# Gate scores folded into existing products, and phase 1 reordered, in a fused conv-and-MoE kernel

## What is computed

```
x: (16, 56, 56, 96) float32
# block 1, on windows of 7x7 tokens, after a layer norm of x over the 96 channels
w  = _ln(windows(_ln_c(x)), ln1_w, ln1_b)
xB = w @ Bm ;  h[t] = xB[t] + h[t-1] @ A   for the 49 places of a window ;  xr = h @ Cm
y  = gelu(_ln(xr, ln2_w, ln2_b) @ W1 + b1) @ W2 + b2          # 96 -> 384 -> 96
x2 = x + xr + y
# block 2: 4 experts, the best 2 of a token
t      = (x2 - mean) / sqrt(var + 1e-5)
scores = t @ gate_w + gate_b                                   # 96 -> 4
probs  = softmax(scores), kept for the top 2, divided by their sum
out    = x2 + sum_e probs_e * (gelu(t @ w1[e] + b1[e]) @ w2[e] + b2[e])
```

## Time and profile before

| | |
|---|---|
| median of three executions | 2178.2 us |
| the profiled execution: its time | 2182.9 us |
| the profiled execution: its span | 2181.2 us |
| granted clock of TensorE, mean | 0.982 |
| PE busy | 2028.1 us (93%) |
| DVE busy | 1606.3 us (74%) |
| ACT busy | 1465.5 us (67%) |
| POOL busy | 1451.7 us (67%) |
| DMA | 272.89 MB, 125 GB/s |

### The profile page before, as it was taken

One profiled execution on the slowest core, in us unless ns is written; L12 is line 12 of the kernel. 1 busy time (PEld: TensorE's weight loads), 2 busy tenths in 40 slices (PEclk: granted clock), 3 DMA queues, 4 the chain that ended last, 5 costly groups with the idle time before them and its releaser, 6 DMA issues.

```text
span 2181.2 us, 39083 instructions
## 1 busy us (share of the span) xinstructions
PE 2028.1 (93%) x10145; PEld 1437.0 (66%) x10145; DVE 1606.3 (74%) x6863; ACT 1465.5 (67%) x2529; POOL 1451.7 (67%) x1286
## 2 busy tenths in 40 slices
PE   3999999999999999999965999999999999999996
PEld 2656565666666666666644777777777777777775
DVE  5677777777777777777744777777777777777775
ACT  3555555545455555555523888988898888898895
POOL 2366666666666666666553777777777777777776
PEclk9999999999999999999976999999999999999998
DMA  4011111121112111111115666676667667666663
GB/s 161 28 54 58 54 50 62 49 63 47 63 47 63 50 60 52 58 54 44 40 43 188 202 215 206 199 216 207 203 207 211 206 201 213 203 207 214 208 203 94
DMA packets 120721, 272.89 MB, mean 125 GB/s; under 512 B 25702, under 2 KB 34303, under 8 KB 120500
## 3 DMA queue, kind: packets, MB, share of 16 engines
q1 hardware_dynamic: 85680, 209.91, 32.4%
q0 software_dynamic: 32000, 58.87, 7.7%
q10 hardware_dynamic: 2820, 1.61, 0.3%
HBM read 204.28 MB, written 66.98 MB: 124 GB/s over the span
## 4 chain that ended last, share of the span: by engine, by line
PE 52%; POOL 20%; DVE 20%; issue 6%; ACT 1%; DMA 1%; ACTq 0%; SPq 0%; POOLq 0%; DVEq 0%
POOL rstd L396 11%; POOL sorted_rows L405 7%; PE mix_ps L1035 7%; PE mix_ps L1033 6%; PE mix_ps L1034 6%; DVE xr_n L625 4%; PE up_ps L1019 3%; PE turn_ps L1019 3%; PE turn_ps L1020 3%; DVE stats L613 3%; PE up_ps L1020 3%; PE turn_ps L1021 3%; PE up_ps L1021 3%; PE tok_ps L1042 3%; DVE y_lo L701 3%
## 5 line engine op out<-in xcount | busy, mean ns | idle before, releaser
L436 POOL DMA_INDIRECT out<-out_sb,idx x412 | 423.8, 1029 | 263.9 <-DVE out_sb L832 155.4
L788 DVE TENSOR_TENSOR g_lo<-g,g_hi 128x512 fp32r<-128x512 f32 x618 | 420.3, 689 | 207.8 <-ACT g_hi L546 117.7
L405 POOL DMA_INDIRECT sorted_rows<-rows,pos x392 | 421.7, 1076 | 114.1 <-issue 99.9
L546 ACT CAST g_hi<-g 128x512 fp32r<-128x512 f32 x618 | 380.9, 616 | 13.1
L485 ACT ACTIVATE g<-up_ps 128x512 f32<-128x512 f32 x294 | 175.6, 597 | 253.3 <-PE up_ps L891 134.5
L425 POOL TENSOR_TENSOR ex<-euler,rows 128x16 f32<-128x16 f32 x103 | 311.9, 3028 | 14.2 <-DMA rows<-sorted_rows 13.0
L900 PE MATMUL y_ps<-g,d_raw 128*96 128x512 f32 x588 | 298.3, 602 | 0.2 <-ACT y_sb L492 0.2
L396 POOL TENSOR_TENSOR rstd<-var_eps,neg_half 128x8 f32<-128x8 f32 x147 | 248.6, 1691 | 12.2
L1033 PE MATMUL mix_ps<-g_hi,ew 128*96 128x512 f32 x618 | 244.5, 396 | 0.5 <-DVE g_lo L788 0.5
L1035 PE MATMUL mix_ps<-g_lo,ew 128*96 128x512 f32 x618 | 244.2, 395 | 0.0
L1034 PE MATMUL mix_ps<-g_hi,ew 128*96 128x512 f32 x618 | 244.0, 395 | 0.0
(11 more groups left out here) (159 smaller groups left out, 4426.7 us busy)
## 6 DMA issues: line engine op xcount, KB each, us to landing
ew<-expert_w SPq DMA_DIRECT2D x206, 384.0 KB
ew<-expert_w SPq DMA_DIRECT2D x206, 288.5 KB
rows<-sorted_rows SPq DMA_DIRECT2D x103, 394.0 KB
x_in<-in_x SPq DMA_DIRECT2D x49, 384.0 KB
out<-out_sb,idx POOLq DMA_INDIRECT x412
sorted_rows<-rows,pos POOLq DMA_INDIRECT x392
sorted_rows<-pad_rows SPq DMA_DIRECT2D x11, 394.0 KB, 10.4
expert_w<-w_hi SPq DMA_DIRECT2D x4, 192.0 KB, 2.6
```

The source lines that it names most:

```text
L405: pool.indirect_dma_start(out=sorted_rows[:, :], out_offset=bass.IndirectOffsetOnAxis(ap=pos[:, r, s:s + 1], axis=0), in_=rows[:, r, s, :] ...
L436: pool.indirect_dma_start(out=out_rows, out_offset=bass.IndirectOffsetOnAxis(ap=idx[:, r, s:s + 1], axis=0), in_=out_sb[:, r, s, :], in_of ...
L546: act.copy(g_hi[:, n % PART_RING, :], g[:, n % G_RING, :]).then_inc(hi_done, 1)
L788: dve.tensor_tensor(g_lo[:, n % PART_RING, :], g[:, n % G_RING, :], f(g_hi[:, n % PART_RING, :]), ALU.subtract).then_inc(lo_done, 1)
```

## The change

It alters phase 1 alone (and the place of columns within a row: x2, then the four scores, then the normalised t, then the number of the token).

- **Scores.** The gate weights, with their mean over channels taken off (`centred_weights`), are multiplied on the chip into Cm, W2, A, Bm and b2 as four more columns: sum_xr gives 104 columns (xr, the scores of xr, and the scores of the normalised x), down and turn_y give 100. VectorE multiplies the scores of x back by the deviation (`dev_x`), sums up (`take_xr`, `add_x2`), multiplies by LN_T's rstd and adds the bias (`gate`). The transposes of the normalised rows, tn_t and the score products are gone.
- **xr in PSUM.** The copy of xr is gone: bn_stats and the adds read mix_ps, and ScalarE normalises xr out of mix_ps (`normalise_xr`). The mix region is free when both have read it.
- **Rows.** Four of the eight sub-tiles are normalised on ScalarE (`normalise_rows`, a period later), four on VectorE.
- **Order.** from_input follows from_state ahead of the ups, sum_xr follows rank; the copy to h_t comes before gelu 0. y_lo comes before add_x2, positions after taking xr.
- **GpSimd.** var_eps is made by VectorE; one power over 16 columns serves LN_X and LN_T; all 8 scatters stand together.
- **Loads.** Eight first loads (with turned_w, Cm and W2 transposed), three for the MLP, two late ones.

```diff
-            def rstd_of(k, t, used):
-                pool.wait_ge(moment_ok[k], t + 1)
...
-                pool.tensor_scalar(var_eps[:, k, :], moment[:, k, :, 1], LN_SCALE[k], LN_EPS[k], ALU.mult, ALU.add).then_inc(
-                    var_ok[k], 1)
...
+            def rstd_of_r(t):
+                pool.wait_ge(var_ok[LN_R], t + 1)
...
+                pool.tensor_tensor(rstd_r[:, t % 2, :], var_eps[:, LN_R, :], neg_half[:, 0, :], ALU.pow).then_inc(rstd_r_ok, 1)
+
+            def rstd_of_x_and_t(t):
...
+                pool.tensor_tensor(rstd_xt[:, t % 2, :, :], var_eps[:, LN_X:, :], neg_half[:, :, :], ALU.pow).then_inc(rstd_xt_ok, 1)
...
-                if tile(p - 1):
-                    rstd_of(LN_T, p - 1, tn_ok)
-                if tile(p + 3):
-                    rstd_of(LN_X, p + 3, x_n_ok)
-                if tile(p - 2):
-                    scatter(p - 2, (0, 1, 2))
-                if tile(p + 1):
-                    rstd_of(LN_R, p + 1, xr_n_ok)
-                if tile(p - 2):
-                    scatter(p - 2, (3, 4, 5, 6, 7))
+                if tile(p + 1):
+                    rstd_of_r(p + 1)
+                if tile(p + 3) or tile(p - 1):
+                    rstd_of_x_and_t(p + 3)
+                if tile(p - 2):
+                    scatter(p - 2, range(SUBS))
...
+            def normalise_xr(t):
+                act.wait_ge(shift_r_ok, t + 1)
+                if t >= 1:
+                    act.wait_ge(xr_turned, t)
+                for s in range(SUBS):
+                    ins = act.activation(xr_n[:, s, :], mix_tok[:, s // HALF_SUBS, s % HALF_SUBS, 0:C], ACT.Identity,
+                                         scale=rstd_r[:, t % 2, s:s + 1], bias=shift_r[:, s:s + 1])
+                ins.then_inc(xr_n_ok, 1)
+
+            def normalise_rows(t):
+                act.wait_ge(shift_t_ok, t + 1)
+                for s in range(HALF_SUBS, SUBS):
...
+                ins.then_inc(t_n_ok, 1)
...
-                    gelu(p, 0)
-                    gelu(p, 1)
                 if tile(p + 2):
                     normalise_x(p + 2, 0)
                 if tile(r):
...
-                    act.copy(h_t[:, :], mix_ps[0:C, :]).then_inc(h_t_ok, 1)
+                    act.copy(h_t[:, :], mix_ps[0:CG, :]).then_inc(h_t_ok, 1)
+                if tile(p):
+                    gelu(p, 0)
+                    gelu(p, 1)
+                if tile(p + 2):
+                    normalise_x(p + 2, 1)
+                if tile(p - 2):
+                    normalise_rows(p - 2)
                 if tile(p):
                     gelu(p, 2)
                     gelu(p, 3)
...
                     copy_y(p, 0)
                     gelu(p, 4)
-                if tile(p - 1):
...
-                    act.copy(tn_t[0:C, :], turn_ps[0:C, :]).then_inc(tn_t_ok, 1)
+                if tile(r):
+                    normalise_xr(r)
                 if tile(p):
                     gelu(p, 5)
...
+            def take_xr(t):
+                dst = x_xr[:, t % 2, :, :].rearrange("p (b s) c -> p b s c", b=2)
...
+                dve.tensor_tensor(dst[:, :, :, C:CG], mix_tok[:, :, :, CG:CGX],
+                                  dev_x[:, t % DEV_RING, :].rearrange("p (b s) -> p b s", b=2).unsqueeze(3).to_broadcast(
+                                      [P, 2, HALF_SUBS, EXPERTS]), ALU.mult).then_inc(in_gate_ok, 1)
+                dve.tensor_tensor(dst[:, :, :, 0:C], mix_tok[:, :, :, 0:C],
+                                  x_in[:, t % X_RING, :, :].rearrange("p (b s) c -> p b s c", b=2), ALU.add)
+                dve.wait_ge(in_gate_ok, t + 1)
+                dve.tensor_tensor(dst[:, :, :, C:CG], mix_tok[:, :, :, C:CG], dst[:, :, :, C:CG], ALU.add).then_inc(x_xr_ok, 1)
...
             for p in periods():
                 r = p + 1
-                if tile(p - 1):
-                    add_x2(p - 1, 1)
                 if tile(p):
                     dve.wait_ge(y_hi_ok, p + 1)
                     dve.tensor_tensor(y_lo[:, :], turn_ps[0:C, :], f(y_hi[0:C, :]), ALU.subtract).then_inc(y_lo_ok, 1)
-                if tile(p - 2):
-                    positions(p - 2)
                 if tile(p - 1):
+                    add_x2(p - 1, 1)
                     dve.wait_ge(x2_ok, 2 * p)
-                    moments(LN_T, p - 1, rows[:, (p - 1) % ROW_RING, :, COL_X2:COL_T])
+                    in_stats(LN_T, p - 1, lambda s: rows[:, (p - 1) % ROW_RING, s, COL_X2:COL_BELOW])
+                    variance(LN_T, p - 1, (rstd_xt_ok, p + 3))
...
                 if tile(r):
                     dve.wait_ge(xr_summed, r + 1)
-                    dve.tensor_copy(xr[:, :, :].rearrange("p (b s) c -> p b (s c)", b=2), mix_tok).then_inc(xr_copied, 1)
-                    dve.wait_ge(xr_copied, r + 1)
-                    moments(LN_R, r, xr)
...
+                    in_stats(LN_R, r, lambda s: mix_tok[:, s // HALF_SUBS, s % HALF_SUBS, 0:C])
+                    variance(LN_R, r, (rstd_r_ok, r))
+                    take_xr(r)
+                    shift_of_r(r)
+                if tile(p - 2):
+                    positions(p - 2)
                 if tile(p):
                     add_x2(p, 0)
-                if tile(r):
-                    if r >= 1:
-                        dve.wait_ge(xr_turned, r)
-                    normalise(LN_R, r, xr_n, xr).then_inc(xr_n_ok, 1)
+                if tile(p + 3) or tile(p - 1):
+                    dve.wait_ge(rstd_xt_ok, p + 4)
+                if tile(p + 3):
+                    shift_of_x(p + 3)
                 if tile(p - 1):
+                    shift_of_rows(p - 1)
                     gate(p - 1)
+                    normalise_rows(p - 1)
...
             def from_state(r):
-                mix.take(pe, h_t_ok, r + 1)
...
                 if r >= 1:
                     pe.wait_ge(h_t_ok, r)
+                    pe.wait_ge(x_xr_ok, r)
+                    pe.wait_ge(xr_n_ok, r)
...
                 if tile(r):
                     from_state(r)
+                    from_input(r)
                 if tile(p):
                     up(p, 0)
                     up(p, 1)
...
                 if tile(r):
-                    from_input(r)
+                    sum_xr(r)
...
-                if tile(p - 1):
-                    turn.take(pe, tn_t_ok, p)
-                    pe.wait_ge(tn_ok, p)
-                    to_channels(rows[:, (p - 1) % ROW_RING, :, COL_T:COL_BELOW]).then_inc(tn_turned, 1)
...
-                if tile(p - 1):
-                    tok.take(pe, score_ok, p)
-                    pe.wait_ge(tn_t_ok, p)
-                    for s in range(SUBS):
-                        ins = pe.matmul(tok_ps[:, EXPERTS * s:EXPERTS * (s + 1)], tn_t[:, sub(s)], gate_aug[:, :],
-                                        start=True, stop=True)
-                    ins.then_inc(scored, 1)
```

More of the change, by code:

```diff
@@ L54 @@
 X_RING = 5
+DEV_RING = 4
 G_RING = 4
@@ L65 @@
 POS_STEPS = 5
-GATE_STEPS = 5
-LN_X, LN_R, LN_T = 0, 1, 2
-LN_SCALE = (1.0 + EPS_1, 1.0, 1.0)
-LN_EPS = (EPS_C * EPS_1, EPS_1, EPS_T)
-FIRST_LOADS, LATER_LOADS = 5, 3
+GATE_STEPS = 7
+LN_R, LN_X, LN_T = 0, 1, 2
+LN_SCALE = (1.0, 1.0 + EPS_1, 1.0)
+LN_EPS = (EPS_1, EPS_C * EPS_1, EPS_T)
+FIRST_LOADS, MLP_LOADS, LATER_LOADS = 8, 3, 2
 PREP_STEPS = 9
+GATE_SUMS = 4
 CONSTS = 21
@@ L491, in copy_y @@
                     act.wait_ge(y_turned, m - 1)
-                act.activation(y_sb[:, m % 2, :], y_ps[0:C, :], ACT.Identity, bias=b2_col[0:C, 0:1]).then_inc(y_copied, 1)
+                if m == 0:
+                    act.wait_ge(gate_sums, GATE_SUMS)
+                act.activation(y_sb[:, m % 2, :], y_ps[0:CG, :], ACT.Identity, bias=b2_col[0:CG, 0:1]).then_inc(y_copied, 1)
             for p in periods():
@@ new lines, in shift_of_rows, with normalise_rows @@
+            def shift_of_rows(t):
+                if t >= 1:
+                    dve.wait_ge(t_n_ok, t)
+                dve.scalar_tensor_tensor(shift_t[:, :], in0=moment[:, LN_T, HALF_SUBS:, 0], scalar=-1.0,
+                                         in1=rstd_xt[:, t % 2, 1, HALF_SUBS:], op0=ALU.mult, op1=ALU.mult).then_inc(shift_t_ok, 1)
+            def normalise_rows(t):
+                for s in range(HALF_SUBS):
+                    ins = dve.tensor_scalar(rows[:, t % ROW_RING, s, COL_T:COL_ID], rows[:, t % ROW_RING, s, COL_X2:COL_BELOW],
+                                            moment[:, LN_T, s, 0:1], rstd_xt[:, t % 2, 1, s:s + 1], ALU.subtract, ALU.mult)
@@ L643, in gate @@
                 r = t % ROW_RING
-                dve.wait_ge(scored, t + 1)
-                dve.tensor_copy(score[:, :, :].rearrange("p s e -> p (s e)"), tok_ps[:, 0:SUBS * EXPERTS]).then_inc(score_ok, 1)
-                dve.wait_ge(score_ok, t + 1)
+                dve.tensor_tensor(score[:, :, :], rows[:, r, :, COL_BELOW:COL_T],
+                                  rstd_xt[:, t % 2, 1, :].unsqueeze(2).to_broadcast([P, SUBS, EXPERTS]), ALU.mult).then_inc(gate_step, 1)
+                after(1)
```

(25 more changed lines are left out.)

222 lines of the change are left out of this document (124 added, 98 removed).

## The result

The changed kernel takes **1977.5 us** in the median of 4 runs (1976.8 to 1978.5), the kernel before 2177.0 (2175.7 to 2178.8): ratio 0.908, 95% interval 0.907 to 0.910. The forecast was 2005 in a range of 1968 to 2058: faster, as said, and by 28 us more. A "turn" is the time from the first up product of one tile to that of the next. The profiled execution after has a span of 1975.1 us and a time of 1976.8.

What follows compares the result with a forecast made beforehand. The prediction took the loop over GpSimd and VectorE as the bound. Start +4, loop -168 (48 turns from 22.01 to 18.5 us) and end -9 gave -173 us, a median of 2005 us, range 1968 to 2058.

Steps and rivals of the forecast that it cites:

- What bounded the kernel before: Tile loop: the loop over GpSimd and VectorE sets the 22.01 us turn; TensorE is full but for 1.7 us.
- TensorE's new work, 17.7 us: TensorE per tile: 20.45 us, less 2.76 removed, plus 0.11 for wider sum_xr, less 0.1, gives 17.7.
- What is late next is the queue of ScalarE: Tile loop after the change: ScalarE's queue makes TensorE wait, giving 18.5 us a turn, 0.8 over TensorE's own 17.7.
- rival (a): Tile loop: TensorE alone is the bound, turn 17.7, 207 us off the loop, 1966 us; chance 0.12.
- The walk, 18.2 us: One turn of TensorE laid against ScalarE's queue, first up to next up, 18.2 us before the handoff margin.
- I add 0.3 for handoffs that the walk rounds off: Margin of 0.3 us put on each turn of the tile loop, giving 18.5 us.
- xr_n at 0.36 us apart: ScalarE's eight normalisations of xr from PSUM taken as 0.36 us apart, bounds 0.34 and 0.45.
- ScalarE's load, 15.2 a turn: ScalarE per tile: load of 11.8 us plus 3.4 for twelve normalisations less the copy of tn, 15.2 in all.
- The order of lateness: Sign to look for in each turn: shift of xr ready before gelu 4 ends, with 0.7 us to spare.
- Start, +4: Before the first up: first from_input at 1.2 GHz and ScalarE's slower normalising cost 4 us.
- End, -9: After the last tile: GpSimd's queue sets the first expert rows, 49 us after the first up against 58.0, saving 9.
- Rival (d): Tile loop: waits lower TensorE's granted clock, making it slower; at a quarter, turn 22.9 and 2216 us; chance 0.03.

Runs made afterwards that it cites:

- b_scat8: Kernel before with the eight scatters of a tile together behind the power of xr, nothing else changed: 2132.7 us, ratio 0.979.
- b_fill: Kernel before without rows transposes, tn_t and score products, with the transposes of x done three times as useless filler: 2166.9 us, ratio 0.995.
- a_order: Changed kernel with the old order of state products on TensorE and of gelus and h_t on ScalarE: 2106.1 us, ratio 0.967 to the kernel before.
- a_extra: Changed kernel with the eight transposes of x done twice: 2016.9 us, ratio 0.927 to the kernel before.
- a_best: Changed kernel with up 5 ahead of down 3 and the first sub-tile of xr normalised on VectorE: 1960.5 us, ratio 0.901 to the kernel before.
- a_one: Changed kernel with only the first sub-tile of xr normalised on VectorE: 1977.3 us, ratio 0.908 to the kernel before.
- a_sbuf: Changed kernel with xr copied to SBUF first, read there by VectorE and ScalarE: 2034.8 us, ratio 0.935 to the kernel before.
- a_swap: Changed kernel with only up product 5 put ahead of down product 3: 1975.3 us, ratio 0.907 to the kernel before.
- b_noscore: Kernel before without transposes of the normalised rows, tn_t and score products; four row channels serve as scores: 2211.9 us, ratio 1.016.
- b_both: Kernel before without rows transposes, tn_t and score products, and with eight scatters together behind the power of xr: 2144.3 us, ratio 0.985.

## Why the prediction was right, and where it was off

**What bounded the kernel before:** right. It is the loop over VectorE and GpSimd (b_scat8: a move in GpSimd's queue shortens every turn; b_fill: TensorE work taken out at full clock does not). That the new order and the removed work pay together is right too (a_order, a_extra).

**TensorE's new work, 17.7 us:** right, 17.62 in a_best.

**"What is late next is the queue of ScalarE":** wrong but for one wait. The prediction has three waits of TensorE for ScalarE, 0.4 to 0.8 us in all. Down 5 does not wait for gelu 5, and the transposes of xr add no wait for x_t. What is there is the wait of down 3 for the copy of y: 0.17 us in the timeline, and 0.36 with the slower restart behind it (two downs take 1.07 us there and 0.86 elsewhere in the chain), which is what separates 17.98 from a_best's 17.62. It is no matter of ScalarE's load: ScalarE itself waits 0.26 us for down 2 before that copy. So TensorE sets the turn, as a_extra shows. The measured turn of 17.98 us lies between rival (a) (17.7, 1966 us) and the forecast's band (18.1 to 19), and the time is nearer to (a), 12 us off, than to the forecast's 2005, 28 us off. One of the two conditions of (a), that the wait at down 5 vanishes, came true. The direction and the range were right because the old bound and TensorE's work were; the mechanism named for the last 0.8 us was not.

**The walk, 18.2 us:** near, measured against the chain. From the first up at 0: first down 3.63 (walk 3.63), down 3 at 8.47 (8.56), transposes of x 10.24 (10.12), of xr 13.18 (13.45), from_state 14.59 (14.67), next up 18.03 (18.2). It took 0.25 us for the wait of down 3, which costs 0.36, and 0.2 for that of down 5, which costs nothing. So part of its closeness is luck.

**The term that was mis-sized most is "I add 0.3 for handoffs that the walk rounds off".** The marks above agree to 0.3 us without any margin. The start-to-start times of the earlier trace rows held TensorE's handoffs already. On the profiled executions the forecast was 2010 and the time 1976.8, 33 us apart: 14 are this 0.3 (48 turns), 11 the 0.22 by which the walk itself was long (18.2 for 17.98), 4 the end, 4 the second phase.

**xr_n at 0.36 us apart:** off by 0.04. Eight take 2.69, so 0.32 apart. What it brings is that down 5 no longer waits for gelu 5, at most 0.2 a turn or 10 us; beyond that there is no gain while down 3 waits, for a_one takes 0.3 us more from the same place and gains nothing. The nearest row, the normalisation from SBUF, was the wrong neighbour: the source counts. By the Trainium skill (VectorE: DVE Perf Modes, the section on the TRN2 errata) ScalarE should be 43 ns faster from PSUM; the pace is 41 ns faster (0.320 against 0.361 in a_sbuf), the durations of single instructions only 7 to 9 (447 for 454 and 456), so it agrees where instructions follow each other. The 17 us that the sum would have got by it are more than the place could give. The same table's 62 cycles more for VectorE is not seen: stats from PSUM 248 ns, from SBUF 246. The +0.2 us taken for those stats is 0.03 (eight take 1.41 us from PSUM and 1.38 from SBUF in a_sbuf).

**ScalarE's load, 15.2 a turn:** 14.4. The sum should read +3.3 and 15.1 by its own terms; the pace of xr_n is 0.3 of the difference, and the rest is not traced to a cause. **The order of lateness** (shift of xr before gelu 4 ends): right, the shift is there 0.87 us before the normalising starts, for the 0.7 said.

**Joined power at 3.0:** 2.89. **Start, +4:** +3.9; but kernels that differ from this one little or not at all at the start have their first up anywhere from 51.6 (a_best) to 54.9 us (a_swap), so the hit is partly luck. **End, -9:** -13.0. GpSimd's queue sets it, as said; it is done with tile 46 (935.59) at 18.2 us after the last tile's first up (917.39), not "near 23", and scatters in a row are 1.27 us apart for the 1.37 taken:

```profile
933.37 0.96 POOL L431 DMA_INDIRECT sorted_rows<-rows,pos  x1 [0.30 <-issue]
934.63 0.96 POOL L431 DMA_INDIRECT sorted_rows<-rows,pos  x1 [0.30 <-issue]
935.60 2.94 POOL L421 TENSOR_TENSOR rstd_xt<-var_eps,neg_half 128x16 f32<-128x16 f32 x1
...
958.64 0.96 POOL L431 DMA_INDIRECT sorted_rows<-rows,pos  x1 [0.30 <-issue]
```

**What the prediction does not have at all:** the move of xr into PSUM frees GpSimd. In the kernel before one GpSimd instruction of each turn stands under VectorE's add of x and is some 0.65 us longer for it (last section); in the kernel after the power under that add keeps its 1.67 us. a_sbuf shows that without this part of the change the time would be 57 us longer; by the waits worked out there, the longer power is the larger part of it.

**Rival (d)** had the wrong kernel but a real mechanism: it is what made b_noscore slower than before. In the kernel after the waits cost 0.36 us a turn, and the clock is 1.00. The Trainium skill (TensorE: Matmul & The Clock Gate, the section on oscillation) warns of it; here the clock stayed at 1.00 with waits of 1.58 and 0.6 us (b_fill) and was 0.96 with 2.4 (b_both) and 0.92 with 3.33 (b_noscore).

## What to carry to other kernels

Lay TensorE's order over one turn, start to start, and walk the other queues against it; that walk was good to 0.2 us in 18, and what had to be left off was a margin for handoffs that the rows already held. A wait in the walk has to be checked for which engine is late: here ScalarE waited for down 2 and TensorE then for ScalarE, at one bank, and neither queue was late. Where a loop over other engines sets the turn, taking work from TensorE buys nothing and can cost its clock: shorten the loop first, or in the same change. Two small waits in a row can hide each other, so that each remedy alone shows nothing and both together pay. Where a source lies can matter to another engine: an add with both sources in SBUF held up GpSimd, the same add with one in PSUM did not.
